# Shifting the start addresses of the matrices that TensorE reads by 32 bytes in a fused four-layer graph network kernel

## The reference

```
L0 (three steps, a gated recurrent unit):  a = adj @ h
    z = sigmoid([a, a] @ w3.T + h @ u3.T + biases)
    r = sigmoid([a, a] @ w4.T + h @ u3.T + biases)
    c = tanh([a, a] @ w5.T + (r * h) @ u5.T + biases)
    h = (1 - z) * h + z * c
L1: rel = adj.T * (x @ wq.T) @ (x @ wk.T).T, rows scaled to length 1;  rel @ (x @ wv.T)
L2: adj @ x @ weight + bias
L3: norm_adj @ (x @ weight) + bias
```

## Time and profile before

| | before |
|---|---|
| median of 3 runs | 1236.61 us (1236.04 to 1237.11) |
| the profiled execution | 1236.37 us |
| its span, first to last instruction | 1234.5 us |
| outside the span | 1.9 us |
| TensorE (PE) busy | 1214.8 us, 98% |
| DVE busy | 1007.9 us, 82% |
| ACT busy | 659.2 us, 53% |
| mean granted TensorE clock | 0.999 of full speed |

### The profile page before, as it was taken

How to read it: one execution, slowest core, us unless ns; L and a number is a source line. 1 busy time by engine, 2 the same in 40 slices (tenths; PEclk the granted TensorE clock), 3 DMA queues, 4 the chain that set the end, 5 groups by cost and what they waited for, 6 DMA issues and landing times.

```text
span 1234.5 us, 21269 instructions
## 1 busy us (share of the span) xinstructions
PE 1214.8 (98%) x7454; PEld 1088.9 (88%) x7454; DVE 1007.9 (82%) x2220; ACT 659.2 (53%) x1179; POOL 220.4 (18%) x447
## 2 busy tenths in 40 slices
PE   8999999999999999999999999999999999999997
PEld 7789899898988989899898998989889898998896
DVE  6679787897878969788797878979789697885899
ACT  5445554555645555555555545556455555554542
POOL 1003021020211203122030210202112031220122
PEclk9999999999999999999999999999999999999999
DMA  7030221302113031120402213022130311300001
GB/s 205 18 86 18 69 69 35 102 0 77 59 34 102 0 100 36 44 92 0 112 24 68 68 34 101 1 70 66 34 102 0 94 42 40 96 1 35 1 2 35
DMA packets 105021, 66.93 MB, mean 54 GB/s; under 512 B 65690, under 2 KB 98468, under 8 KB 104996
## 3 DMA queue, kind: packets, MB, share of 16 engines
q1 hardware_dynamic: 104784, 66.08, 18.1%
q0 software_dynamic: 192, 0.52, 0.2%
q10 hardware_dynamic: 20, 0.01, 0.0%
HBM read 35.13 MB, written 23.07 MB: 47 GB/s over the span
## 4 chain that ended last, share of the span: by engine, by line
PE 82%; DVE 10%; POOL 4%; issue 3%; DMA 1%; ACT 0%; DVEq 0%; SPq 0%; POOLq 0%; ACTq 0%
PE b_ps L515 34%; PE f_ps L515 27%; PE f_ps L510 12%; PE b_ps L510 7%; POOL b_rstd L425 2%; DVE normed L1694 2%; PE f_ps L677 2%; DVE hb_feat L1583 1%; DVE f_cand L1577 1%; POOL b_var_eps L423 1%; DVE b_ps L1715 1%; DVE b_stats L1678 1%; DVE b_rh_lo L1720 1%; PE b_ps L741 1%; DVE b_moments L1685 1%
## 5 line engine op out<-in xcount | busy, mean ns | idle before, releaser
L423 POOL TENSOR_TENSOR b_var_eps<-b_moments,eps 128x2 f32<-128x2 f32 x120 | 39.8, 332 | 955.8 <-DVE b_moments L1685 955.8
L425 POOL TENSOR_TENSOR b_rstd<-b_var_eps,neg_half 128x2 f32<-128x2 f32 x120 | 93.4, 778 | 9.4
L1103 ACT ACTIVATE f_gate<-f_ps,bias_r 128x512 f32<-128x512 f32 x66 | 45.4, 690 | 83.6 <-PE f_ps L515 83.6
L1063 ACT ACTIVATE b_a_hi<-normed 128x512 fp32r<-128x512 f32 x60 | 37.9, 631 | 88.6 <-DVE normed L1694 88.3
L1115 ACT ACTIVATE f_cand<-f_ps,bias_c 128x512 f32<-128x512 f32 x66 | 45.3, 686 | 61.2 <-PE f_ps L515 61.2
L1561 DVE TENSOR_TENSOR f_gate<-f_gate,hf_feat 128x512 f32<-128x512 f32 x66 | 45.6, 690 | 32.4 <-ACT f_gate L1103 30.7
L1063 ACT ACTIVATE b_rh_hi<-b_ps 128x512 fp32r<-128x512 f32 x90 | 53.0, 589 | 31.6 <-PE b_ps L515 31.6
L515 PE MATMUL f_ps<-adjT_hi,hf_node_hi 128*128 128x256 f32 x264 | 67.6, 289 | 1.1 <-DVE hb_node_lo L1614 1.0
L515 PE MATMUL f_ps<-adjT_lo,hf_node_hi 128*128 128x256 f32 x264 | 66.1, 283 | 0.0
L1720 DVE TENSOR_TENSOR b_rh_lo<-b_ps,b_rh_hi 128x512 fp32r<-128x512 f32 x90 | 61.0, 678 | 6.1 <-ACT b_rh_hi L1063 6.1
L1561 DVE TENSOR_TENSOR b_gate<-b_gate,hb_feat 128x512 f32<-128x512 f32 x30 | 20.8, 692 | 54.0 <-ACT b_gate L1103 54.0
(11 more groups left out here) (340 smaller groups left out, 4325.9 us busy)
## 6 DMA issues: line engine op xcount, KB each, us to landing
x_front<-in_x SPq DMA_DIRECT2D x16, 512.0 KB, 4.1
x_blocks<-in_x SPq DMA_DIRECT2D x60, 128.0 KB, 3.0
input_t<-hf_feat SPq DMA_DIRECT2D x15, 512.0 KB, 2.9
turn_sum<-normed SPq DMA_DIRECT2D x14, 512.0 KB, 2.7
result<-turn_sum SPq DMA_DIRECT2D x56, 128.0 KB, 2.9
turn_f<-f_gate SPq DMA_DIRECT2D x14, 512.0 KB, 2.7
f_z<-turn_f SPq DMA_DIRECT2D x56, 128.0 KB, 2.8
out<-result SPq DMA_DIRECT2D x14, 512.0 KB, 3.2
```

The lines of the kernel that those rows point to most:

```text
L423: pool.tensor_tensor(Y.var_eps[:, g], Y.moments[:, g, :, 1], eps[:], ALU.add).then_inc(Y.s_var, 1)
L425: pool.tensor_tensor(Y.rstd[:, g], Y.var_eps[:, g], neg_half[:], ALU.pow).then_inc(Y.s_rstd, 1)
L1063: return act.activation(dst, src, ACT.Copy)
L1103: act.activation(L.gate[:, k], L.ps0[:, k], ACT.Sigmoid, bias=bias_r[:, k:k + 1]).then_inc(L.s_r, 1)
```

## The change

It only reorders the allocations and puts four unused small tensors between them (96, 32, 32 and 32 bytes). No instruction is added, removed or moved.

```diff
-        adjT = split_matrix("adjT")
-        norm_adjT = split_matrix("norm_adjT")
+        wvT = split_matrix("wvT")
+        wqk = split_matrix("wqk")
+
+        shift_96 = sb("shift_96", [P, 24])
         w34T = split_matrix("w34T")
         w4T = split_matrix("w4T")
         w5T = split_matrix("w5T")
         u3T = split_matrix("u3T")
         u5T = split_matrix("u5T")
-        wvT = split_matrix("wvT")
-        wqk = split_matrix("wqk")
-        w2s = split_matrix("w2s")
-        w3s = split_matrix("w3s")
+        shift_back_96 = sb("shift_back_96", [P, 8])
...
+        shift_32 = sb("shift_32", [P, 8])
+        adjT = split_matrix("adjT")
+        norm_adjT = split_matrix("norm_adjT")
+        w2s = split_matrix("w2s")
+        w3s = split_matrix("w3s")
+        sum_split = sb("sum_hi", [P, C, T], F32R), sb("sum_lo", [P, C, T], F32R)
+        rel_split = nodes("rel_hi", F32R), nodes("rel_lo", F32R)
+        shift_back = sb("shift_back", [P, 8])
+
         main = Layers(sb, sem, "b", back, per_graph, input_t, s_input_t, 0,
-                      (sb("sum_hi", [P, C, T], F32R), sb("sum_lo", [P, C, T], F32R)), nodes("normed"), nodes("result"),
-                      (nodes("v_hi", F32R), nodes("v_lo", F32R)), (nodes("rel_hi", F32R), nodes("rel_lo", F32R)),
+                      sum_split, nodes("normed"), nodes("result"),
+                      (nodes("v_hi", F32R), nodes("v_lo", F32R)), rel_split,
                       sb("sq_sum", [P, G, N]), True)
```

## The result

The changed kernel takes 1244.26 us (median of 4 runs, 1242.69 to 1244.45) against 1236.38 us before; the ratio is 1.0058, 95% interval 1.0043 to 1.0073. **It is slower by 0.6%**, 7.2 us by the ratio. The forecast was 1198 us.

What follows compares the result with a forecast made beforehand. It took PE to bound the kernel, with 13.3 ns on each of 7104 float32r matmuls. Half of that, 47.4 us, times 82% gave 1236.4 - 38.9 = 1197.5, said as 1198 us; likeliest 1180 to 1215, 8 in 10 1162 to 1241.

Steps and rivals of the forecast that it cites:

- The bound on PE, the chain and the two steps: PE busy 1214.8 of 1234.5 us, 82% of the path; float32r matmuls take 226.7 ns (512 columns), 120.0 (256).
- I take half the surcharge: Float32r matmuls: 6.7 of 13.3 ns saved on each of 7104, 47.4 us of PE time.
- The largest gain: Upper bound for the float32r matmuls: surcharge falls to 2.3 ns, 11 x 7104 = 78 us.
- All of it goes: Rival: surcharge falls to 2.3 ns in every product, 64 us gained, 1172 us; chance 0.12.
- Nothing moves: Rival: the matmul surcharge is structural, time stays 1236.4 us (1234 to 1239); chance 0.23.
- the shift costs: Rival: shifted weight loads and moving reads touch a fifth 128-byte piece, 3.3 ns a matmul, 1256 us; chance 0.17.
- Only one family gains: Rival: say only the GRU matmuls (2880 of 7104) gain, by half, 16 us, 1221 us; chance 0.20 with small part.
- The share that reaches the end: 82% of the PE saving counted, 38.9 us; PE waits longer for hb_feat and f_cand before the L677 transposes.
- DVE and DMAs cost nothing to speak of: Shifted tiles cost DVE nothing (bound 3 us); DMAs of normed and result stay hidden, at most 9 us.
- POOL's small operations: POOL and the small statistics tensors move by multiples of 32 bytes; their few-element instructions cost nothing.
- A distance ends part of the collisions: Moving and stationary streams walking the same banks in step collide less when starts differ; gain from nothing to 78 us.

Runs made afterwards that it cites:

- the eighth run: Kernel before with reset matmuls cut into 128 columns and update into 256, GRU weights at 96 past a multiple of 128; 1373.35 us.
- the fourth experiment: Kernel before with one 32-byte tensor in front of everything, so all tiles shift together; 1237.37 us, ratio 1.0003.
- the first experiment: Changed kernel with the five GRU weights put back on a multiple of 128; 1228.55 us, ratio to before 0.9937.
- the second: Kernel before with only the five GRU weights moved, to 96 past a multiple of 128; 1250.0 us, ratio 1.0109.
- seventh: Kernel before with reset matmuls cut into 128 columns and update into 256, GRU weights at distance 0; 1371.09 us.
- tenth: Kernel before with reset matmuls cut into 384 and 128 columns, update into 320 and 192, all distances 0; 1291.55 us.

## Why the prediction was wrong

- **The bound on PE, the chain and the two steps** (226.7 and 120.0 ns) were read rightly, and addresses do act on the steps: 5.3 of the 7.9 us are there, and most of the rest is the clock and a DMA wait.
- **The step that failed is "I take half the surcharge"**, 6.7 ns off each of 7104 matmuls. The sign was taken to be one for all products, and the sum was 47.4 us off PE. Measured, at distance 32: -2.8 ns on most 256-column steps and +5.4 ns on the 512-column ones, together 5.3 us on top. The 6.7 ns came from the earlier trace rows, a step behind a run of 512 columns at distance 0, which tells nothing of other distances. I had rows for both lengths side by side and saw that both pay 32 cycles; that made one rule look safe, and hid that it was one distance only.
- **The largest gain was bounded wrongly.** I took 2.3 ns as the floor from the float32 row. The two cycles a column that it rests on do show: in the profile before, 128-column float32 transposes step at 109 ns (median, L677) and the 256-column products of the earlier trace rows at 216, 0.84 ns for each further column; and at half the clock, in the eighth run, 128 float32 columns (L687) and 256 float32r ones (L517) both step at 213 to 214 ns. But in a step of 216 ns a load of the 111 ns estimated above has room. At 256 float32r columns (106.7 ns, 256 x 0.417) the load would be the floor, by the same estimate, 4 ns above bare streaming; no distance could then have brought the whole 11 ns. Keys at 64 came to 113.3, the cheap step of the earlier trace rows: half the surcharge exists, in one product.
- **"All of it goes"** fell with this. **"Nothing moves"** fell too, though its time, 1236, was nearer than the forecast: the even mean in the earlier trace rows was that of one distance, and said nothing of others.
- **The rival "the shift costs"** had the right side, 1256 for a measured 1244, but not its mechanism: the side was luck. A fifth 128-byte piece is touched by every load of the fourth experiment, which costs nothing (1.0003), and by the 256-column pieces of the eighth, which gain.
- **"Only one family gains"** was nearest in kind, with the families the wrong way round: the GRU ones lose.
- **The share that reaches the end** (82%) was 75% in the first experiment, in part for the reason named: PE waits longer for hb_feat.
- **DVE and DMAs cost nothing to speak of**, as said: L1715, now L1723, has a median of 696 ns instead of 692, DVE is busy for 0.5 us more, and the DMAs of rows 10 take 2.7, 3.0 and 3.2 us. POOL's small operations were put at nothing, but its busy time rose by 9.3 us: b_neg_mean takes 335 ns instead of 221, b_var_eps 390 instead of 332, b_shift 423 instead of 495. So it does in the first experiment, which is faster, and not in the second; the cause wasn't looked for.
- **"A distance ends part of the collisions"** is shown in its effect alone. A shift of moving against stationary tiles changes the steps: 117.3 ns at 256 columns in the first experiment and 233.2 at 512 in the second, against 119.8 and 227.7 before. A common shift doesn't (fourth: 119.8 and 227.8). What in the memory makes it, collisions or something else, no run shows.

## What to carry to other kernels

Where float32r matmuls follow each other without pause, look at the distance between the streaming operand and the weights loaded beside it, modulo 256 bytes rather than 128, and measure it for each length apart: here equal starts were best at 512 columns (227.7 ns against 230.4 to 233.3, with one exception) and a distance of 32 was best, or near it, at 256 (116.8 to 118.1 against 119.8). A surcharge that is equal in two rows is not one mechanism; before pricing a change on it, ask what both rows have in common, here distance 0. A layout change of this kind costs no instruction, so it is best tried one family at a time in a single profile and read by the steps. And before a difference of 0.1% or so is put down to a change, look at the granted clock of both profiles: here 3.4 us at half the clock were worth 1.4 us.

## What the runs showed of the hardware that was not expected

- 128-column float32r matmuls, each with a weight load of 128 columns, step at 110.6 ns at distance 0 and at +32 (48 in 5.31 us, seventh and eighth run), and 192-column ones at 112 (tenth). I estimate the load at about 111 ns from this, and take it for the bound at these two lengths.
- At distance 0, 256-column steps are 120.0 ns for whole stretches; at +32 they scatter (mix: 113 to 124) around 117.
- 8 bytes of distance cost both lengths (values 121.2 ns at +8, w5T 232 ns at -8); 64 bytes gave 113.3 ns in keys only, in three layouts 113.3 to 113.8, and 117 to 118 in the other products. Why keys alone is open. Keys changes its stationary tile from step to step under the same moving one, mix its moving one over the same stationary one; that wasn't tried apart.
- The granted clock fell to half (0.50) for 3.4 us some 54 us into the span of the changed kernel, worth 1.4 us; the profile of the kernel before lacks this and that of the fourth experiment, with the same steps, has it.
